# VectorE turns one more unit, xD of the first x is made from SBUF alone, and the loads of x and T are cut and ordered differently

## The chip, the cores and the metric

The kernel runs on one core of a Trainium2 chip. The metric is the device time of one execution in microseconds. Of the kernel before there are three timed runs, at 103.55, 103.83 and 106.04 us, with a median of 103.83 us, and one profiled execution at 103.36 us.

## The reference

```python
def reference(x, itok_B_1_98, L0_cond_T):       # x: 8 x 512 x 512, T: 100 x 512 x 512, float32
    def _L0_cond_ref(x, fwd_steps, T):
        Tb = T[fwd_steps - 1]                    # one matrix of T for each of the 8 batches
        return jnp.einsum('bij,bjk->bik', Tb, x)
    x = x + _L0_cond_ref(x, itok_B_1_98, L0_cond_T)
    return x
```

For each of eight batches one matrix of a table T is picked by a token, a float32 product of 512 x 512 x 512 is formed, and x is added.

## The kernel before, in words

**Units.** A batch is cut into N = 4 units of 128 output rows; unit U is batch U // 4, block U % 4. There are 32 units. For each unit TensorE needs the block of T transposed (its weights), and it multiplies it with all of x of the batch (four matmuls with 512 moving columns for each product).

**Three products.** To keep float32 accuracy with the type fp32r, x and T are split. xH is x rounded (ScalarE), xL = x - xH, and xD = xH - 4096 xL. TH is T / 4096 rounded, TL = T - 4096 TH and TD = TH - TL. A unit takes `multiply_high` (TH times xH into the bank `same`), `multiply_low` (TL times xL into the same bank) and `multiply_diff` (TD times xD into the bank `diff`, which ScalarE has filled before from `same`, called `seed`). VectorE then subtracts `diff` from x (`sum_up`). So a unit is 12 matmuls of 512 columns.

**Who makes what.** ScalarE makes xH (L213; L201 for the first x), TH (`cut_T`, L234; `cut_T_pair`, L241), the seeds (L249), and a copy of xH in PSUM, `xH_copy` (L219), from which VectorE makes xD (L353), so that VectorE reads one SBUF and one PSUM tensor there. VectorE makes xL of the first x (L339), all TL (L370 for unit 0, L376, L382), xD, and the sums (L390). GpSimd makes all TD (L312, L320) and xL of every later half x (L304). Turning (transposing) a block of T is done by TensorE for units 0 to 3 (`BY_PE = N`; L435, L446), as four transposes of 128 x 128, and by VectorE from unit 4 on (L360). VectorE's transpose only works within 32 x 32 quadrants, so T for these units is loaded in four pieces of 64 KB for each block (`load_T`, L160), which puts the quadrants in their places; the blocks that TensorE turns are loaded as they are (L156).

**The order.** It is written out by hand, a list for each engine, and semaphores tie the lists together. After the first units come steps k = 1 to 15, a step being two units: TensorE does high 2k, low 2k, diff 2k-1, high 2k+1, low 2k+1, diff 2k. In step k VectorE turns units 2k+2 and 2k+3 (for k > 1), makes xD of half x number k+1, sums up unit 2k-1, makes TL of pair k+1, and sums up unit 2k. ScalarE in a step: a seed, xH of half k+2, TH of pair k+1, a seed, `xH_copy`. GpSimd: xL of half k+2, TD of pair k+1.

**The loads.** Issued by SyncE (queue SP): T of batch 0 in three DMAs (blocks 0, 1, and 2 with 3 together), the first half of the second x (L148), then, once the tokens have landed in SBUF, blocks 0 and 1 of T of batch 1 in eight DMAs, the other half of the second x, the other eight DMAs of T of batch 1, and T of batch 2. ScalarE's queue carries the first x in three DMAs, the tokens, from the third x on whole x of 1 MB (L144, one in every second step), and the stores (L165).

**Around the start.** TensorE first multiplies with an identity matrix (L426, L428) until the first block of T is there. All waits of later work are on counts of semaphores, such as `TL_ready`, `xD_ready`, `turned_by_pe`.

## Time and profile before

| | |
|---|---|
| profiled execution | 103.36 us |
| its span, first to last instruction | 101.6 us |
| median of the three timed runs | 103.83 us |
| granted TensorE clock | 1.00 of full speed, in every slice |
| TensorE busy | 96.5 us, 95% of the span |
| VectorE busy | 87.0 us, 86% |
| GpSimd busy | 72.6 us, 71% |
| ScalarE busy | 65.3 us, 64% |
| DMA queue of SP, of ScalarE | 37.1% and 41.6% of 16 engines' span |

Busy time of TensorE counts matmuls, which overlap each other; the chain that ended last tells better what the end hangs on. The first 20 us, where the engines start one after another, are where the lists differ from the steady steps.

### The profile page before, as it was taken

The numbers are of one execution on the slowest core, as the hardware profiler recorded it, in microseconds if no ns is written. First come the engines' busy times: TensorE is split into PE (matmuls) and PEld (weight loads), VectorE is DVE, ScalarE is ACT, GpSimd is POOL, SyncE is SP. The second block draws the span as 40 slices with busy tenths as digits, with TensorE's granted clock in tenths as the row PEclk, the third lists the DMA queues.
The fourth block names the chain that finished last, engine by engine and source line by source line (L and its number), as shares of the span: only waits on it lengthen the run. The fifth ranks groups of instructions, "written<-read, shape, count | busy, mean of one in ns | idle before, by whom it ended". The sixth has DMA issues, their size and how long they took to land.

```text
span 101.6 us, 1827 instructions
## 1 busy us (share of the span) xinstructions
PE 96.5 (95%) x440; PEld 80.7 (79%) x440; DVE 87.0 (86%) x101; ACT 65.3 (64%) x87; POOL 72.6 (71%) x38
## 2 busy tenths in 40 slices
PE   3999999999999999999999999999999999999950
PEld 3997888888888888888888888888888888888840
DVE  0075989999999999999999999999999999993250
ACT  0766588758596876858585858596876858362100
POOL 2001369999979797988979797979797988908100
PEclk9999999999999999999999999999999999999999
DMA  1989996999999787998999899998989630405064
GB/s 46 306 219 416 276 282 131 319 283 335 343 329 322 238 252 238 336 315 244 292 364 300 213 324 313 246 323 219 357 272 335 213 126 26 181 3 206 6 275 138
DMA packets 20749, 25.30 MB, mean 249 GB/s; under 512 B 2306, under 2 KB 16898, under 8 KB 19970
## 3 DMA queue, kind: packets, MB, share of 16 engines
q10 hardware_dynamic: 3602, 15.34, 41.6%
q1 hardware_dynamic: 17136, 9.84, 37.1%
q8 instruction: 4, 0.07, 0.3%
q14 instruction: 7, 0.06, 0.2%
HBM read 16.78 MB, written 8.39 MB: 248 GB/s over the span
## 4 chain that ended last, share of the span: by engine, by line
PE 94%; DVE 1%; POOL 1%; issue 0%; POOLq 0%
PE same L461 29%; PE same L472 29%; PE diff L483 28%; PE diff L426 4%; PE same L428 3%; PE turned L446 1%; DVE out_sb L417 1%; DVE out_sb L390 1%; PE turned L435 0%; POOL eye L298 0%; POOL eye L296 0%; PE same L435 0%; POOLq L298 0%; POOLq L523 0%
## 5 line engine op out<-in xcount | busy, mean ns | idle before, releaser
L304 POOL TENSOR_TENSOR xL<-x_sb,xH 128x1024 fp32r<-128x1024 f32 x14 | 33.7, 2409 | 7.2 <-ACT xH L213 7.2
L320 POOL TENSOR_TENSOR TD_r<-TH_r,TL 128x1024 fp32r<-128x1024 f32 x14 | 33.7, 2407 | 2.9 <-issue 2.9
L472 PE MATMUL same<-xL,TL 128*128 128x512 f32 x128 | 34.4, 391 | 0.0
L461 PE MATMUL same<-xH,TH_r 128*128 128x512 f32 x128 | 34.4, 390 | 0.0
L483 PE MATMUL diff<-xD,TD_r 128*128 128x512 f32 x124 | 33.1, 389 | 0.0
L249 ACT ACTIVATE diff<-same 128x512 f32<-128x512 f32 x31 | 18.1, 583 | 22.3 <-PE same L472 22.1
L360 DVE STREAM_TRANSPOSE turned<-T_sb 128x512 f32<-128x512 f32 x28 | 29.3, 1090 | 0.2
L461 PEld LDWEIGHTS same<-xH,TH_r 128*128 128x128 f32 x128 | 23.9, 188 | 5.3 <-ACT TH_r L234 0.2
L472 PEld LDWEIGHTS same<-xL,TL 128*128 128x128 f32 x128 | 23.9, 188 | 4.9
L483 PEld LDWEIGHTS diff<-xD,TD_r 128*128 128x128 f32 x124 | 23.3, 188 | 4.8
L390 DVE TENSOR_TENSOR out_sb<-x_sb,diff 128x512 f32<-128x512 f32 x31 | 20.8, 671 | 4.0 <-PE diff L483 4.0
L353 DVE SCALAR_TENSOR_TENSOR xD<-xL,xH_copy 128x1024 fp32r<-128x1024 f32 x15 | 18.0, 1201 | 0.6 <-ACT xH_copy L219 0.6
L382 DVE SCALAR_TENSOR_TENSOR TL<-TH_r,turned 128x1024 fp32r<-128x1024 f32 x14 | 16.9, 1210 | 0.0
L219 ACT ACTIVATE xH_copy<-xH 128x1024 f32<-128x1024 f32 x15 | 15.4, 1024 | 0.0
L213 ACT ACTIVATE xH<-x_sb 128x1024 fp32r<-128x1024 f32 x14 | 14.8, 1055 | 0.3 <-DMA x_sb<-x 0.3
L241 ACT ACTIVATE TH_r<-turned 128x1024 fp32r<-128x1024 f32 x14 | 14.3, 1021 | 0.5 <-POOL TD_r L320 0.5
L312 POOL TENSOR_TENSOR TD_r<-TH_r,TL 128x512 fp32r<-128x512 f32 x4 | 5.2, 1294 | 10.7 <-DVE TL L370 8.4
L339 DVE TENSOR_TENSOR xL<-x_sb,xH 128x512 fp32r<-128x512 f32 x4 | 2.7, 690 | 5.6 <-ACT xH L201 5.5
L426 PE MATMUL diff<-eye 128*128 128x128 f32 x16 | 3.8, 431 | 1.5 <-POOL eye L298 1.5
L426 PEld LDWEIGHTS diff<-eye 128*128 128x128 f32 x16 | 3.5, 330 | 1.5 <-POOL eye L298 1.5
L428 PEld LDWEIGHTS same<-eye 128*128 128x128 f32 x20 | 3.4, 263 | 0.0
L428 PE MATMUL same<-eye 128*128 128x128 f32 x20 | 3.3, 341 | 0.0
(29 smaller groups left out, 20.7 us busy)
## 6 DMA issues: line engine op xcount, KB each, us to landing
out<-out_sb ACTq DMA_DIRECT2D x15, 512.0 KB, 5.9
T_sb<-T SPq DMA_DIRECT2D x112, 64.0 KB, 4.2
x_sb<-x ACTq DMA_DIRECT2D x6, 1024.0 KB, 7.4
x_sb<-x SPq DMA_DIRECT2D x2, 512.0 KB, 7.1
x_sb<-x ACTq DMA_DIRECT2D x2, 256.0 KB, 3.7
x_sb<-x ACTq DMA_DIRECT2D x1, 512.0 KB, 4.6
T_sb<-T SPq DMA_DIRECT2D x2, 256.0 KB, 5.5
T_sb<-T SPq DMA_DIRECT2D x1, 512.0 KB, 6.5
```

What stands on the lines that cost most here:

```text
L213: nc.scalar.activation(half(xH, h), x_sb[b % X_SLOTS][:, i:i + 2], COPY, scale=LEAN).then_inc(xH_ready, 2)
L219: nc.scalar.activation(xH_copy[:], half(xH, h).bitcast(fp32), COPY).then_inc(xH_copied, 1)
L249: nc.scalar.activation(diff[U % 2][:], same[U % 2][:], COPY, scale=-(RADIX + 1.0)).then_inc(seeded, 1)
L304: nc.gpsimd.tensor_tensor(half(xL, h), x_sb[b % X_SLOTS][:, i:i + 2], half(xH, h).bitcast(fp32), ALU.subtract).then_inc(xL_ready, 2)
L320: nc.gpsimd.tensor_tensor(TD_r[s][:], TH_r[s][:].bitcast(fp32), TL[s][:].bitcast(fp32), ALU.subtract).then_inc(TD_ready, 2)
L353: nc.vector.scalar_tensor_tensor(half(xD, h), half(xL, h).bitcast(fp32), -RADIX, high, ALU.mult, ALU.add).then_inc(xD_ready, 2)
L360: nc.vector.transpose(turned[:, U % 2].rearrange("p u (m q) -> p m u q", q=Q), T_sb[b % T_SLOTS][:, n].rearrange("p (m c u) -> p m u c", c ...
L382: nc.vector.scalar_tensor_tensor(TL[s][:], TH_r[s][:].bitcast(fp32), -RADIX, turned[:], ALU.mult, ALU.add).then_inc(TL_ready, 2)
L390: nc.vector.tensor_tensor(out_sb[b % OUT_SLOTS][:, n], x_sb[b % X_SLOTS][:, n], diff[U % 2][:], ALU.subtract).then_inc(sum_ready, 1)
L461: nc.tensor.matmul(same[U % 2][:], TH_r[p][:, i, j], xH[s][:, j], start=(j == 0), stop=False)
L472: done = nc.tensor.matmul(same[U % 2][:], TL[p][:, i, j], xL[s][:, j], start=False, stop=(j == N - 1))
L483: done = nc.tensor.matmul(diff[U % 2][:], TD_r[p][:, i, j], xD[s][:, j], start=False, stop=(j == N - 1), skip_group_check=True)
```

## The change

- `BY_PE` goes from 4 to 3: unit 3 is turned by VectorE (`turn(3)`), no longer by TensorE. TensorE's transposes of unit 2 now stand before `multiply_high(1)`.
- Block 3 of T of batch 0 is therefore loaded in four pieces of 64 KB; blocks 0, 1 and 2 are three DMAs of 256 KB.
- VectorE makes xD of the first x from xL and xH, both in SBUF, in three instructions (blocks 0, 1, and 2 with 3), the first two between its xL. ScalarE no longer copies xH of half 0 to PSUM.
- GpSimd's first TD also waits until all of the first xD is made.
- VectorE sums up unit 0 before it turns unit 5.
- x from the third on is loaded by halves of 512 KB, one in each step, with a semaphore for each half of a slot.
- The four pieces of a block of T are issued in the order 0, 2, 1, 3.

```diff
-    BY_PE = N
+    BY_PE = N - 1
...
             if b == 0:
-                return {0: (1, 1), 1: (2, 1), 2: (N, 1)}
+                return {0: (1, 1), 1: (2, 1), 2: (3, 1), 3: (N, G)}
             return {n: (n + 1, G) for n in range(N)}
...
-        def load_x(eng, b):
-            eng.dma_start(x_sb[b % X_SLOTS][:], x_part[b]).then_inc(x_loaded[b % X_SLOTS], 16)
-
-        def load_second_x(eng, i):
-
-            eng.dma_start(x_sb[1][:, 2 * i:2 * i + 2], x_part[1, :, 2 * i:2 * i + 2]).then_inc(half_x_loaded[i], 16)
+        def load_x_half(eng, h):
+            b, i = h // 2, h % 2
+            eng.dma_start(x_sb[b % X_SLOTS][:, 2 * i:2 * i + 2], x_part[b, :, 2 * i:2 * i + 2]
+                          ).then_inc(half_x_loaded[b % X_SLOTS][i], 16)
...
-                for g in range(G):
+                for g in [0, 2, 1, 3]:
...
             cut_first_T()
-            copy_xH_half(0)
             cut_T(1)
...
-            load_x(act, 2)
+            load_x_half(act, 4)
             for k in range(1, PAIRS):
...
-                if k % 2 == 0 and b + 2 < B:
+                if k + 4 < 2 * B:
                     if b >= 2:
                         act.wait_ge(sum_ready, (b - 1) * N)
-                    load_x(act, b + 2)
+                    load_x_half(act, k + 4)
...
                 pool.wait_ge(TL_ready, U + 1)
-                if U == 1:
-
-                    pool.wait_ge(xD_ready, N)
+
+                pool.wait_ge(xD_ready, N)
...
+            def first_xD(u, end):
+                dve.wait_ge(xH_ready, end)
+                dve.wait_ge(first_xL_ready, end)
+                nc.vector.scalar_tensor_tensor(xD[0][:, u:end], xL[0][:, u:end].bitcast(fp32), -RADIX,
+                                               xH[0][:, u:end].bitcast(fp32), ALU.mult, ALU.add).then_inc(xD_ready, end - u)
...
-            for u in range(N):
-                first_xL(u)
+            first_xL(0)
+            first_xL(1)
+            first_xD(0, 1)
+            first_xL(2)
+            first_xL(3)
+            first_xD(1, 2)
             cut_first_T()
-            cut_x_half(0)
+            first_xD(2, 4)
             cut_T(1)
-            cut_x_half(1)
+            turn(3)
             cut_T(2)
             turn(4)
             cut_T(3)
+            sum_up(0)
             turn(5)
-            sum_up(0)
...
             multiply_low(0)
+            turn(2)
             multiply_high(1)
-            turn(2)
-            turn(3)
             multiply_low(1)
```

Three places show what moves. The first is TensorE, from the first product of unit 0 to the first `multiply_diff`. L461 (L457 in the changed kernel) is `multiply_high`, L446 (L442) a turn, L472 (L468) `multiply_low`, L483 (L479) `multiply_diff`. Before:

```order
L461 MATMUL same<-xH,TH_r 128x512 x4
L446 MATMUL turned<-eye,T_sb 128x128 x4
L472 MATMUL same<-xL,TL 128x512 x4
L461 MATMUL same<-xH,TH_r 128x512 x4
L446 MATMUL turned<-eye,T_sb 128x128 x8
L472 MATMUL same<-xL,TL 128x512 x4
L483 MATMUL diff<-xD,TD_r 128x512 x4
```

Changed (here with the semaphores that an instruction waits for):

```order
L457 MATMUL same<-xH,TH_r 128x512 [waits xH_ready,first_TH_ready] x2
L457 MATMUL same<-xH,TH_r 128x512 [waits xH_ready,TH_ready] x2
L442 MATMUL turned<-eye,T_sb 128x128 [waits TL_ready,T_loaded0_1]
L442 MATMUL turned<-eye,T_sb 128x128 x3
L468 MATMUL same<-xL,TL 128x512 [waits first_xL_ready,TL_ready]
L468 MATMUL same<-xL,TL 128x512 [waits first_xL_ready] x3
L442 MATMUL turned<-eye,T_sb 128x128 [waits TL_ready,T_loaded0_2]
L442 MATMUL turned<-eye,T_sb 128x128 x3
L457 MATMUL same<-xH,TH_r 128x512 [waits TH_ready] x4
L468 MATMUL same<-xL,TL 128x512 [waits TL_ready]
L468 MATMUL same<-xL,TL 128x512 x3
L479 MATMUL diff<-xD,TD_r 128x512 [waits xD_ready,TD_ready,seeded]
```

Four of the twelve transposes behind unit 0 are gone, and the four of unit 2 stand one product earlier.

The second place is VectorE at the start. Before:

```order
L339 TENSOR_TENSOR xL0<-x_sb0,xH0 128x512 [waits xH_ready] x4
L370 SCALAR_TENSOR_TENSOR TL0<-TH_r0,turned 128x128 [waits first_TH_ready]
L370 SCALAR_TENSOR_TENSOR TL0<-TH_r0,same1 128x128 [waits first_TH_ready]
L370 SCALAR_TENSOR_TENSOR TL0<-TH_r0,turned 128x256 [waits TH_ready]
L353 SCALAR_TENSOR_TENSOR xD0<-xL0,xH_copy 128x1024 [waits xH_copied,first_xL_ready]
L376 SCALAR_TENSOR_TENSOR TL0<-TH_r0,turned 128x512 [waits TH_ready]
L353 SCALAR_TENSOR_TENSOR xD0<-xL0,xH0 128x1024 [waits first_xL_ready]
L376 SCALAR_TENSOR_TENSOR TL1<-TH_r1,turned 128x512 [waits TH_ready]
L360 STREAM_TRANSPOSE turned<-T_sb1 128x4x4x32 [waits TL_ready,T_loaded1_0]
```

Changed:

```order
L331 TENSOR_TENSOR xL0<-x_sb0,xH0 128x512 [waits xH_ready] x2
L337 SCALAR_TENSOR_TENSOR xD0<-xL0,xH0 128x512 [waits first_xL_ready,xH_ready]
L331 TENSOR_TENSOR xL0<-x_sb0,xH0 128x512 [waits xH_ready] x2
L337 SCALAR_TENSOR_TENSOR xD0<-xL0,xH0 128x512 [waits first_xL_ready,xH_ready]
L362 SCALAR_TENSOR_TENSOR TL0<-TH_r0,turned 128x128 [waits first_TH_ready]
L362 SCALAR_TENSOR_TENSOR TL0<-TH_r0,same1 128x128 [waits first_TH_ready]
L362 SCALAR_TENSOR_TENSOR TL0<-TH_r0,turned 128x256 [waits TH_ready]
L337 SCALAR_TENSOR_TENSOR xD0<-xL0,xH0 128x1024 [waits first_xL_ready,xH_ready]
L368 SCALAR_TENSOR_TENSOR TL0<-TH_r0,turned 128x512 [waits TH_ready]
L352 STREAM_TRANSPOSE turned<-T_sb0 128x4x4x32 [waits TL_ready,T_loaded0_3]
L368 SCALAR_TENSOR_TENSOR TL1<-TH_r1,turned 128x512 [waits TH_ready]
L352 STREAM_TRANSPOSE turned<-T_sb1 128x4x4x32 [waits TL_ready,T_loaded1_0]
```

Half of xD now stands ahead of the first TL, none waits for ScalarE's copy, and one more transpose stands in front of that of unit 4.

The third place is the queue of SP at its start. Before:

```order
L156 DMA T_sb0<-T 128x512
L156 ISA
L156 DMA T_sb0<-T 128x1024
L148 DMA x_sb1<-x 128x1024
L170 TENSOR_LOAD itok_sb
L160 ISA x2
```

Changed (`TENSOR_LOAD` reads the token, `ISA` is arithmetic of the sequencer):

```order
L153 DMA T_sb0<-T 128x512
L157 ISA
L157 DMA T_sb0<-T 32x4x128
L157 ISA
L157 DMA T_sb0<-T 32x4x128
L157 ISA
L157 DMA T_sb0<-T 32x4x128
L157 ISA
L157 DMA T_sb0<-T 32x4x128
L144 DMA x_sb1<-x 128x1024
L167 TENSOR_LOAD itok_sb [waits itok_loaded]
L157 ISA x2
```

Four more DMAs stand in front of the second x and of all of T from batch 1 on.

## Rows read from the trace of the kernel before

**Rows 1.** The page, part 4: share of the span on the chain that ended last.
```profile
PE 94%; DVE 1%; POOL 1%; issue 0%; POOLq 0%
```

**Rows 2.** The chain of waits, 0 to 20 us: start us, us, engine, tile, line, count.
```profile
10.13 0.53 PE turned L446 x4
...
12.55 0.95 PE turned L446 x8
```

**Rows 3.** Timeline, the first units: start us, us, engine, line, operation, [idle before, releaser].
```profile
6.94 1.29 DVE L339 TENSOR_TENSOR xL<-x_sb,xH 128x512 fp32r<-128x512 f32 x2 [0.56 <-ACT xH L201]
...
8.91 0.29 DVE L370 SCALAR_TENSOR_TENSOR TL<-TH_r,turned 128x128 fp32r<-128x128 f32 x1 [0.67 <-ACT TH_r L227]
...
9.24 1.02 ACT L219 ACTIVATE xH_copy<-xH 128x1024 f32<-128x1024 f32 x1
9.38 0.42 DVE L370 SCALAR_TENSOR_TENSOR TL<-TH_r,turned 128x256 fp32r<-128x256 f32 x1
...
9.91 0.56 PEld L446 LDWEIGHTS turned<-eye,T_sb 128*128 128x128 f32 x4 [0.22 <-issue]
...
12.14 1.22 DVE L353 SCALAR_TENSOR_TENSOR xD<-xL,xH 128x1024 fp32r<-128x1024 f32 x1
...
13.50 1.30 POOL L312 TENSOR_TENSOR TD_r<-TH_r,TL 128x512 fp32r<-128x512 f32 x1 [2.33 <-DVE xD L353]
...
14.47 1.12 DVE L360 STREAM_TRANSPOSE turned<-T_sb 128x512 f32<-128x512 f32 x1
...
14.76 2.41 POOL L304 TENSOR_TENSOR xL<-x_sb,xH 128x1024 fp32r<-128x1024 f32 x1
```

**Rows 4.** Timeline of SP's queue, 0 to 26 us: when its DMAs were issued.
```profile
4.34 0.60 SPq L148 DMA_DIRECT2D x_sb<-x  x1
6.84 4.03 SPq L160 DMA_DIRECT2D T_sb<-T  x8
10.92 0.42 SPq L148 DMA_DIRECT2D x_sb<-x  x1
```

**Rows 5.** Waits of SP's queue.
```profile
SPq L170 <- DMA itok_sb<-itok: 0.8, 1, 0.8
```

**Rows 6.** SP's DMAs issued 4.2 to 5 and 10.9 to 11.3 us: KB, us to landing.
```profile
x_sb<-x SPq DMA_DIRECT2D x1, 512.0 KB, 8.4
...
x_sb<-x SPq DMA_DIRECT2D x1, 512.0 KB, 5.8
```

**Rows 7.** SP's T pieces issued 6.5 to 8.6 and 8.7 to 10.9 us.
```profile
T_sb<-T SPq DMA_DIRECT2D x4, 64.0 KB, 4.6
...
T_sb<-T SPq DMA_DIRECT2D x5, 64.0 KB, 3.6
```

**Rows 8.** The page, part 6: the later x, KB, median us to landing.
```profile
x_sb<-x ACTq DMA_DIRECT2D x6, 1024.0 KB, 7.4
```

**Rows 9.** Timeline, 16 to 27 us: the second x and the pairs behind it.
```profile
16.79 1.06 ACT L213 ACTIVATE xH<-x_sb 128x1024 fp32r<-128x1024 f32 x1 [0.28 <-DMA x_sb<-x]
...
18.39 2.41 POOL L304 TENSOR_TENSOR xL<-x_sb,xH 128x1024 fp32r<-128x1024 f32 x1
18.55 1.02 ACT L241 ACTIVATE TH_r<-turned 128x1024 fp32r<-128x1024 f32 x1
...
19.68 1.22 DVE L382 SCALAR_TENSOR_TENSOR TL<-TH_r,turned 128x1024 fp32r<-128x1024 f32 x1
...
20.77 1.28 POOL L312 TENSOR_TENSOR TD_r<-TH_r,TL 128x512 fp32r<-128x512 f32 x1
...
21.30 0.87 PEld L472 LDWEIGHTS same<-xL,TL 128*128 128x128 f32 x4
...
22.21 0.87 PEld L483 LDWEIGHTS diff<-xD,TD_r 128*128 128x128 f32 x4
...
25.20 1.22 DVE L382 SCALAR_TENSOR_TENSOR TL<-TH_r,turned 128x1024 fp32r<-128x1024 f32 x1
...
26.74 0.87 PEld L472 LDWEIGHTS same<-xL,TL 128*128 128x128 f32 x4
```

More of the change, by code:

```diff
@@ L70, in cond_resid @@
         itok_loaded = sem("itok_loaded")
-        x_loaded = [sem(f"x_loaded{s}") for s in range(X_SLOTS)]
+        half_x_loaded = [[sem(f"half_x_loaded{s}_{i}") for i in range(2)] for s in range(X_SLOTS)]
         first_x_loaded = [sem(f"first_x_loaded{i}") for i in range(len(FIRST_X))]
-        half_x_loaded = [sem(f"half_x_loaded{i}") for i in range(2)]
         T_loaded = [[sem(f"T_loaded{s}_{n}") for n in range(N)] for s in range(T_SLOTS)]
@@ L177, in _ @@
             load_T(sp, t, 0)
-            load_second_x(sp, 0)
+            load_x_half(sp, 2)
             sp.wait_ge(itok_loaded, 16)
@@ L181, in _ @@
             load_T(sp, t, 1, range(2))
-            load_second_x(sp, 1)
+            load_x_half(sp, 3)
             load_T(sp, t, 1, range(2, N))
@@ L204, in cut_x_half @@
                 b = h // 2
-                if b == 1:
-                    act.wait_ge(half_x_loaded[h % 2], 16)
-                else:
-                    act.wait_ge(x_loaded[b % X_SLOTS], 16 * ((b - 2) // X_SLOTS + 1))
+                act.wait_ge(half_x_loaded[b % X_SLOTS][h % 2], 16 * (b // X_SLOTS + (1 if b % X_SLOTS else 0)))
                 if b >= X_SETS:
@@ L216, in copy_xH_half @@
                 act.wait_ge(xH_ready, 2 * h + 2)
-                if h:
-                    act.wait_ge(xD_ready, 2 * h)
+                act.wait_ge(xD_ready, 2 * h)
                 nc.scalar.activation(xH_copy[:], half(xH, h).bitcast(fp32), COPY).then_inc(xH_copied, 1)
@@ L340, in first_xL @@
                                         ).then_inc(first_xL_ready, 1)
-            def cut_x_half(h):
-                if h < 2:
-                    dve.wait_ge(first_xL_ready, 2 * h + 2)
-                else:
-                    dve.wait_ge(xL_ready, 2 * h - N + 2)
-                if h != 1:
-                    dve.wait_ge(xH_copied, max(h, 1))
+            def first_xD(u, end):
[3 more added lines that the diff above has]
+                                               xH[0][:, u:end].bitcast(fp32), ALU.mult, ALU.add).then_inc(xD_ready, end - u)
+            def cut_x_half(h):
+                dve.wait_ge(xL_ready, 2 * h - N + 2)
+                dve.wait_ge(xH_copied, h - 1)
                 if h // 2 >= X_SETS:
                     dve.wait_ge(diff_ready, (h // 2 - X_SETS + 1) * N)
-                high = half(xH, h).bitcast(fp32) if h == 1 else xH_copy[:]
-                nc.vector.scalar_tensor_tensor(half(xD, h), half(xL, h).bitcast(fp32), -RADIX, high,
+                nc.vector.scalar_tensor_tensor(half(xD, h), half(xL, h).bitcast(fp32), -RADIX, xH_copy[:],
                                                ALU.mult, ALU.add).then_inc(xD_ready, 2)
```

## The prediction

> **What bounds the kernel now.** I read the page's part 4 first: 94% of the span lies on TensorE [rows 1], so time goes only where TensorE's chain gets shorter or gets a gap. Then the chain in order of time, from the first product on: behind unit 0 it is products and transposes without a gap, and the transposes stand in it with 0.53 us for four and 0.95 us for eight [rows 2]. Once the steps run, a product of four matmuls takes 0.91 us (21.30 to 22.21) and a step of two units 5.44 us (21.30 to 26.74) [rows 9]. Third, the timeline of the first 27 us, to see how close the other engines are behind TensorE. They are close. TL of the pair that begins at 19.68 is ready at 20.90, and TensorE loads it at 21.30, so 0.40 us of slack. TD of unit 3 is ready at 22.05 and loaded at 22.21: 0.16 us. TL of the next pair is ready at 26.42 and loaded at 26.74: 0.32 us [rows 9]. VectorE needs 5.52 us from one pair's TL to the next (19.68 to 25.20) [rows 9], that is, it has nothing to spare against TensorE's 5.44: what it is late at the start stays. So the gain on TensorE counts only as far as VectorE and GpSimd follow within these slacks.
>
> **The change part by part.**
>
> *Transposes of unit 3 leave TensorE.* Half of the eight: 0.95 / 2 = 0.47 us off the chain, no more than that, since nothing else on TensorE changes. Moving unit 2's transposes ahead of `multiply_high(1)` costs nothing and gives ScalarE's TH of unit 1 more time. The row for this price is that of the chain, 0.12 us for each transpose. The Trainium skill (TensorE: Matmul & The Clock Gate, Part 4: PE-mode transpose) puts a transpose at about 275 ns in a kernel's context, which as an estimate would make the gain 4 x 0.275 = 1.1 us; the chain shows 0.12 us, because consecutive transposes overlap, and the measurement decides.
>
> *VectorE's start.* Two xD instructions of 512 columns come in between the xL. Nearest rows: an xL of that width is 1.29 / 2 = 0.65 us, and the xD of twice the width is 1.22 us [rows 3], so 0.65 us each. The first fits in the idle 0.56 us ahead of 6.94, the second in the 0.67 us ahead of 8.91 [rows 3], each with up to 0.1 us left over. The first TL piece starts about 0.1 us later, and TensorE's transposes of unit 1 wait for the last of them (0.42 us from 9.38, then 0.22 us of idle at TensorE before 9.91) [rows 3]. Cost on the chain: 0.1 us (bounds 0 and 0.2). The remaining xD of 1.22 us ends at about 9.9 + 1.2 = 11.1.
>
> *ScalarE's copy goes*, 1.02 us [rows 3], beside the chain. It moves nothing by itself, since what follows it waits for TensorE.
>
> *GpSimd.* TD of unit 0 now waits for the xD, so it runs 11.1 to 12.4 (1.30 us each [rows 3]) and TD of unit 1 to 13.7, where it ended at 14.80 before, held back by an xD that VectorE made at 12.14 [rows 3]. `multiply_diff(0)` comes at 12.55 + 0.95 + 0.91 = 14.4 before and about 14.0 now, so the later TD of unit 0 is covered by 1.6 us. GpSimd is free for xL of the second x 1.1 us earlier than 14.76.
>
> *VectorE turns unit 3*: 1.12 us more [rows 3], after TL of unit 1. From 11.1: TL of unit 1 to 12.0, the turn to 13.1, TL of unit 2 to 13.8, so the turn of unit 4 could begin at 13.8 instead of 14.47 [rows 3]. But its T arrives later, see next. I take 14.3. The sum of unit 0 ahead of the turn of unit 5 lets ScalarE's seed of unit 2 go without a wait; it changes no total.
>
> *The queue of SP.* Four DMAs more at 4.03 / 8 = 0.50 us each [rows 4]. The second x's first half is issued at 4.34 + 2.0 = 6.35. Before, 1.90 us lay between the end of that issue (4.94) and 6.84, of which 0.8 us were the wait for the tokens [rows 4, 5], which have landed by 6.95 now; so the pieces of T of batch 1 start at 6.95 + 1.1 = 8.05, 1.2 us later, and so does the second half of x, at 12.1. A latency of 4.6 us [rows 7] puts the last piece of unit 4's block (issued at 9.6) at 14.2.
> When do the halves of x land? Not before their old times, 4.34 + 8.4 = 12.7 and 10.92 + 5.8 = 16.7, since the same bytes stand ahead in the queue; not after the old latencies from the new issues, 14.75 and 17.9 [rows 4, 6]. The latency of T's pieces fell from 4.6 to 3.6 us while the queue drained [rows 7]: a later issue meets a shorter queue. I take 13.3 for the first (8.4 us is mostly queue) and 17.2 for the second (5.8 us is less so).
> The first half at 13.3 gives xH at 14.4, and GpSimd starts its xL 0.3 us before the old 14.76: harmless.
> The second half at 17.2 is the term that counts. xH is made 17.3 to 18.3, a seed of 0.5 us follows (in the trace before, xH ended at 17.85 and TH of the pair began at 18.55, with a wait in between [rows 9]), TH of the pair 18.8 to 19.9, TL from 19.9 instead of 19.68: VectorE 0.2 us late. GpSimd's xL of that half starts at 18.4 as before, and TD of unit 3 again ends at 22.05 [rows 9].
>
> *x by halves from the third x on.* Before, 1 MB landed 7.4 us after its issue [rows 8]. Each half is issued two steps, some 10.9 us, before ScalarE cuts it; cover 3.5 us, cost nothing. Six or seven more issues lie on ScalarE's queue, beside its instructions. *The order 0, 2, 1, 3* of pieces that are waited for together: nothing; if it disturbed the DMA engines, the same cover pays.
>
> **The sum.** TensorE gains 0.47 - 0.1 = 0.37 us up to the first steps. Then it meets what did not get earlier: TD of unit 3 at 22.05 against 22.21 - 0.37 = 21.84 is a gap of 0.2 us, and TL of the second pair, 26.42 + 0.2 = 26.62 against 26.74 - 0.37 = 26.37, makes it 0.25 us in all. What stays is 0.1 to 0.2 us, 0.15. On the profiled execution that is 103.36 - 0.15 = 103.2. This execution is 0.47 us below the median of the runs (one of them stands apart at 106.04); the mean of it and the two lower runs is 103.58, and the forecast of the timed median is 103.58 - 0.15 = 103.4.
>
> **The rivals.**
>
> *The whole gain arrives.* If the second half of x lands by 16.8, all of ScalarE and VectorE is on time or earlier (VectorE had 0.6 us in hand at unit 4), and TensorE keeps 0.4 to 0.47 us: 103.1. For it: the bytes ahead in the queue are the same. Against: T's pieces need SP's issue, at 0.50 us for 64 KB.
>
> *The loads of x come too late: slower.* With the old latency of 5.8 us the second half lands at 17.9; xH to 19.1, TH from 19.6 to 20.6, TL from 20.6, 0.95 us behind the old 19.68. TensorE had 0.32 us in hand for it, so the whole kernel is 0.63 us later than before: 103.58 + 0.6 = 104.2. The point from which it decides: with TL more than 0.32 us late, that is x later than 17.3, the kernel is slower than before. If the first half also keeps its 8.4 us, it lands at 14.75, xH ends at 15.9, GpSimd is 1.1 us late, less its slack of 0.16: 104.5. For it: four more DMAs stand in front. Against: the queue was emptying. The Trainium skill (DMA: Bandwidth & Descriptors, the table of measured HBM-to-SBUF transfers) speaks for this rival: it has 138 GB/s at 64 KB against 341 GB/s at 1 MB, which for a block of 256 KB would be an estimated 1.1 us more, and it advises batches of 1 MB.
>
> *Nothing arrives.* VectorE, not TensorE, becomes the clock, because its 5.5 us of a step is what counts once TensorE waits for TL: between 0 and 0.15 us of gain is lost again, 103.6.
>
> *Several at once*, or T of unit 5 late too, in front of all of VectorE's list: over 2 us slower, above 105.7; no row points to it.
>
> **How the numbers follow.** Chances: forecast 0.50, whole gain 0.21, x late 0.20, nothing arrives 0.05, several at once 0.03, and 0.01 for a gain above 2 us, which no row allows (TensorE gives up 0.47 us of work). 2% of the time, about what a measurement of this kernel can tell from no change, is 2.1 us, so all of the first four are "within": 0.96; faster 0.01; slower 0.03. The range takes in the whole gain with the spread between runs (103.1 - 0.2 = 102.9) and most of the late x (104.3); the forecast's own range is 103.1 to 103.7.
>
> **What would show it.** Right: 8 transposes L442 instead of 12; the first part of the chain 0.3 to 0.4 us shorter up to `multiply_diff(0)`; a gap of about 0.2 us of TensorE before TD of unit 3 or TL of a pair between 20 and 27 us; the second half of x at ScalarE at 17.0 to 17.4. The wait of ScalarE for that half, 0.28 us before [rows 9], longer. Wrong: a TensorE with no gap and an end 0.45 us earlier, or ScalarE waiting a microsecond for x and a chain that goes through it.

## The result, and the profile after

The changed kernel is slower: a median of 104.51 us in 13 runs (103.65 to 105.32) against 103.82 us in 13 runs of the kernel before (103.33 to 106.04), a ratio of 1.0061 with a 95% interval of 1.0036 to 1.0087. The forecast was 103.4 us with a range to 104.3. One of its rivals, the loads of x that come too late, gave 104.2 us by the mechanism that is the nearest to what happened. Ratios, here and in the experiments, compare the runs that lie within about 1.5% of the fastest of the same kernel. The profiled execution took 104.61 us, with a span of 102.5 us against 101.6.

The page, part 4, of the changed kernel: the chain that ended last is no longer TensorE's alone.

```profile
PE 75%; SPq 9%; DMA 6%; issue 2%; ACT 2%; DVE 2%; ACTq 0%; DVEq 0%
```

Before, 94% of it was TensorE [rows 1]. Here is the piece where it leaves TensorE, from the chain in order of time, 0 to 24 us (start us, us, what; SPq is the queue of SP, a DMA's time is that from issue to landing):

```profile
11.65 0.32 SPq L157
11.97 0.05 issue
12.02 6.09 DMA x_sb<-x
18.15 0.04 issue
18.19 0.41 ACT xH L208
...
19.19 0.55 ACT diff L243
19.74 0.95 ACT TH_r L235
20.74 0.04 issue
20.79 1.23 DVE TL L374
22.02 0.04 issue
22.06 1.19 PE same L468 x4
```

Read from the bottom: TensorE waits for TL of the second pair, VectorE for ScalarE's TH, ScalarE was held by xH of the second x's second half, that by its DMA, and the DMA by SP's issues. SP's queue, from the timeline (start us, us, count):

```profile
4.45 2.08 SPq L157 DMA_DIRECT2D T_sb<-T  x4
...
6.58 0.42 SPq L144 DMA_DIRECT2D x_sb<-x  x1
...
8.14 3.83 SPq L157 DMA_DIRECT2D T_sb<-T  x8
...
12.02 0.42 SPq L144 DMA_DIRECT2D x_sb<-x  x1
```

These stand 2.2, 1.3 and 1.1 us later than in [rows 4], as forecast. What they did to the engines, from the timeline, 9 to 27 us ([idle before, releaser] at the end):

```profile
9.94 1.22 DVE L337 SCALAR_TENSOR_TENSOR xD<-xL,xH 128x1024 fp32r<-128x1024 f32 x1
10.14 0.56 PEld L442 LDWEIGHTS turned<-eye,T_sb 128*128 128x128 f32 x4 [0.22 <-issue]
...
11.31 2.56 POOL L304 TENSOR_TENSOR TD_r<-TH_r,TL 128x512 fp32r<-128x512 f32 x2 [9.83 <-DVE xD L337]
...
12.35 1.12 DVE L352 STREAM_TRANSPOSE turned<-T_sb 128x512 f32<-128x512 f32 x1
...
14.98 1.13 DVE L352 STREAM_TRANSPOSE turned<-T_sb 128x512 f32<-128x512 f32 x1 [0.94 <-DMA T_sb<-T]
15.04 2.41 POOL L297 TENSOR_TENSOR xL<-x_sb,xH 128x1024 fp32r<-128x1024 f32 x1 [1.18 <-ACT xH L208]
...
18.19 1.06 ACT L208 ACTIVATE xH<-x_sb 128x1024 fp32r<-128x1024 f32 x1 [1.38 <-DMA x_sb<-x]
...
19.40 2.40 POOL L297 TENSOR_TENSOR xL<-x_sb,xH 128x1024 fp32r<-128x1024 f32 x1 [0.70 <-DVE xD L345]
19.68 1.00 ACT L235 ACTIVATE TH_r<-turned 128x1024 fp32r<-128x1024 f32 x1
19.79 0.76 PEld L479 LDWEIGHTS diff<-xD,TD_r 128*128 128x128 f32 x4 [0.64 <-ACT diff L243]
...
20.75 0.76 PEld L457 LDWEIGHTS same<-xH,TH_r 128*128 128x128 f32 x4 [0.21 <-issue]
20.79 1.22 DVE L374 SCALAR_TENSOR_TENSOR TL<-TH_r,turned 128x1024 fp32r<-128x1024 f32 x1 [0.81 <-ACT TH_r L235]
...
22.06 0.76 PEld L468 LDWEIGHTS same<-xL,TL 128*128 128x128 f32 x4 [0.55 <-DVE TL L374]
...
23.16 0.76 PEld L479 LDWEIGHTS diff<-xD,TD_r 128*128 128x128 f32 x4 [0.34 <-issue]
...
26.24 1.22 DVE L374 SCALAR_TENSOR_TENSOR TL<-TH_r,turned 128x1024 fp32r<-128x1024 f32 x1
```

Against [rows 9]: xH of the second half begins at 18.19 instead of 16.79, TL of the second pair at 20.79 instead of 19.68, TensorE loads it at 22.06 instead of 21.30. Four gaps of TensorE (0.64, 0.21, 0.55, 0.34 us of weight-load idle) take back the 0.47 us and more. From there on the two run in step: the next pair's TL is at 26.24 instead of 25.20, the span ends 0.9 us later.

Not all of these 0.9 us belong to the change, since TensorE's first product also begins later. Its first and last weight loads behind the identity matrix, before:

```profile
8.92 0.77 PEld L461 LDWEIGHTS same<-xH,TH_r 128*128 128x128 f32 x4 [0.19 <-ACT TH_r L227]
...
97.23 0.55 PEld L493 LDWEIGHTS same<-xD,TD_r 128*128 128x128 f32 x4
```

and in the changed kernel:

```profile
9.15 0.77 PEld L457 LDWEIGHTS same<-xH,TH_r 128*128 128x128 f32 x4 [0.20 <-ACT TH_r L221]
...
98.11 0.55 PEld L489 LDWEIGHTS same<-xD,TD_r 128*128 128x128 f32 x4
```

The first product begins between 8.74 and 9.79 us in the profiles of this document, in changed and unchanged kernels alike, so 0.23 us of the difference is scatter. From the first product to the last weights it is 88.31 us before and 88.96 after, 0.65 us more. This stretch is used below to compare single profiles.

What the DMA engines did meanwhile shows in windows. Those of the kernel before (the last three columns: granted clock, mean busy share of the 16 DMA engines, which can exceed 1 where transfers overlap, GB/s):

```profile
8.00:10.00 2.00, 2.00 (x13) 1.47 (x12) 1.13 (x4) 1.41 (x4) 0.12 (x1) 1.00 1.04 426
...
16.00:18.00 2.00, 2.00 (x11) 1.65 (x10) 1.90 (x4) 1.57 (x2) 2.00 (x2) 1.00 0.49 111
8.00:16.00 8.00, 8.00 (x44) 6.58 (x44) 6.29 (x10) 5.80 (x11) 3.79 (x3) 1.00 1.08 308
```

and of the changed one:

```profile
8.00:10.00 2.00, 1.89 (x11) 1.31 (x9) 1.64 (x6) 0.74 (x3) 0.00 (x0) 1.00 1.14 286
...
16.00:18.00 2.00, 2.00 (x10) 1.68 (x9) 2.00 (x4) 0.81 (x1) 2.00 (x2) 1.00 1.16 219
8.00:16.00 8.00, 7.89 (x40) 6.33 (x39) 6.20 (x10) 4.59 (x10) 3.52 (x3) 1.00 1.13 263
```

The engines are busy from 8 to 16 us in both, but deliver 308 GB/s before and 263 after. Before, they have caught up by 16 to 18 us (share 0.49); after, they have not (1.16). The issues differ as well as the sizes, so these rates alone do not say which of the two lowered them.

### The profile page after: what moved, and what is told of

The parts are those of the page before. It is cut to its first block, busy times and chain, and to the rows that moved or that the text cites. A ratio compares the mean times of both kernels' runs of the same rounds, so it can differ in the third digit from the quotient of the medians.

```text
span 102.5 us, 1843 instructions
## 1 busy us (share of the span) xinstructions
PE 96.9 (95%) x436; PEld 80.0 (78%) x436; DVE 87.8 (86%) x103; ACT 64.2 (63%) x86; POOL 73.0 (71%) x38
## 4 chain that ended last, share of the span: by engine, by line
PE 75%; SPq 9%; DMA 6%; issue 2%; ACT 2%; DVE 2%; ACTq 0%; DVEq 0%
PE same L468 25%; PE diff L479 25%; PE same L457 24%; DMA x_sb<-x 6%; SPq L157 5%; SPq L167 2%; SPq L153 2%; DVE TL L374 1%; ACT TH_r L235 1%; PE diff L489 1%; ACT diff L243 1%; PE same L489 0%; SPq L144 0%; DVE out_sb L413 0%; ACT xH L208 0%
## 5 line engine op out<-in xcount | busy, mean ns | idle before, releaser
L468 PE MATMUL same<-xL,TL 128*128 128x512 f32 x128 | 34.5, 391 | 0.1
L457 PE MATMUL same<-xH,TH_r 128*128 128x512 f32 x128 | 34.5, 392 | 0.0
L479 PE MATMUL diff<-xD,TD_r 128*128 128x512 f32 x124 | 33.4, 391 | 0.2 <-ACT diff L243 0.2
L352 DVE STREAM_TRANSPOSE turned<-T_sb 128x512 f32<-128x512 f32 x29 | 30.6, 1103 | 1.0 <-DMA T_sb<-T 0.9
L468 PEld LDWEIGHTS same<-xL,TL 128*128 128x128 f32 x128 | 23.9, 188 | 5.4 <-DVE TL L374 0.5
L457 PEld LDWEIGHTS same<-xH,TH_r 128*128 128x128 f32 x128 | 23.8, 188 | 5.2 <-issue 0.2
L479 PEld LDWEIGHTS diff<-xD,TD_r 128*128 128x128 f32 x124 | 23.1, 188 | 5.7 <-ACT diff L243 0.6
L382 DVE TENSOR_TENSOR out_sb<-x_sb,diff 128x512 f32<-128x512 f32 x31 | 21.4, 691 | 3.9 <-PE diff L479 3.9
L374 DVE SCALAR_TENSOR_TENSOR TL<-TH_r,turned 128x1024 fp32r<-128x1024 f32 x14 | 17.2, 1229 | 0.8 <-ACT TH_r L235 0.8
L345 DVE SCALAR_TENSOR_TENSOR xD<-xL,xH_copy 128x1024 fp32r<-128x1024 f32 x14 | 17.1, 1222 | 0.0
L235 ACT ACTIVATE TH_r<-turned 128x1024 fp32r<-128x1024 f32 x14 | 14.3, 1020 | 0.6 <-POOL TD_r L312 0.6
L213 ACT ACTIVATE xH_copy<-xH 128x1024 f32<-128x1024 f32 x14 | 14.3, 1023 | 0.0
```

Of the source, the lines that this page charges most:

```text
L235: nc.scalar.activation(TH_r[p % T_SETS][:], turned[:], COPY, scale=LEAN / RADIX).then_inc(TH_ready, 2)
L345: nc.vector.scalar_tensor_tensor(half(xD, h), half(xL, h).bitcast(fp32), -RADIX, xH_copy[:], ALU.mult, ALU.add).then_inc(xD_ready, 2)
L352: nc.vector.transpose(turned[:, U % 2].rearrange("p u (m q) -> p m u q", q=Q), T_sb[b % T_SLOTS][:, n].rearrange("p (m c u) -> p m u c", c ...
L374: nc.vector.scalar_tensor_tensor(TL[s][:], TH_r[s][:].bitcast(fp32), -RADIX, turned[:], ALU.mult, ALU.add).then_inc(TL_ready, 2)
L382: nc.vector.tensor_tensor(out_sb[b % OUT_SLOTS][:, n], x_sb[b % X_SLOTS][:, n], diff[U % 2][:], ALU.subtract).then_inc(sum_ready, 1)
L457: nc.tensor.matmul(same[U % 2][:], TH_r[p][:, i, j], xH[s][:, j], start=(j == 0), stop=False)
```

## The experiments

Each was timed against the kernel before on the same chip; the groups ran on different chips, so a ratio of one group set against one of another is less certain than within a group. Theory A: the four added DMAs make the second x late. Theory B: VectorE's longer list at the start holds TensorE. Theory C: the later halves of x or the order of the pieces disturb the whole run. Theory D came after the first two groups: it is what the DMA engines deliver, not SP's issue.

**Which part carries the loss.** The first run takes the part on unit 3 out of the change, the second does it alone.

```diff
# a1_unit3_back, on the changed kernel; TensorE's turn(3) behind multiply_high(1)
-    BY_PE = N - 1
+    BY_PE = N
-                return {0: (1, 1), 1: (2, 1), 2: (3, 1), 3: (N, G)}
+                return {0: (1, 1), 1: (2, 1), 2: (N, 1)}
-            turn(3)              # VectorE
# a2_unit3_alone, on the kernel before: the same lines the other way round
```

> The changed kernel with unit 3 turned by TensorE again (T of batch 0 in three DMAs, the last of 512 KB; eight transposes on TensorE behind unit 0), all else as changed. Theory A (the four added DMAs ahead of the second x make its second half land at 18.1 instead of 16.7, and ScalarE, which waits for it in order, makes everything behind it late): the second half lands at 16.6 to 16.9 again, TensorE has no gap between 19 and 24 us, and the time is that of before, ratio 0.997 to 1.001. Theory B (VectorE's list at the start is too long: xD from SBUF in three instructions, the sum before the turn): TL of the second pair begins later than 19.8 though x is in time, ratio 1.003 or more. Theory C (the later x by halves, or the order of the pieces, disturbs the DMA engines for the whole run): ratio 1.004 or more, with gaps behind 30 us.

> The kernel before with this part alone: unit 3 turned by VectorE, its block loaded in four pieces of 64 KB. Theory A: the whole loss is here, the second half of the second x lands at about 18, ScalarE waits 1.2 to 1.5 us for it, TL of the second pair begins at 20.6 to 20.9, ratio 1.004 to 1.009. Theory B: the loss needs the changed xD; ratio 0.998 to 1.002. Theory C: the same as B.

Measured: 0.9999 (0.9964 to 1.0035) without the part, 1.0060 (1.0015 to 1.0106) with it alone. So the whole loss belongs to the part on unit 3, and for xD from SBUF, the halves of the later x, the order of the pieces and of the sum together nothing is measured. Theory C falls, and B in the form that blames the new xD. In the profile of a2, ScalarE waits for the second half until 18.84 and VectorE's TL of the second pair begins at 21.43, later than the 20.6 to 20.9 expected. One caution: in a1's profile ScalarE waited for that half until 17.52, not the 16.6 to 16.9 expected. Single landings scatter by more than half a microsecond from one execution to the next, so one landing proves little and the timed runs have to be weighed with it.

**The added DMAs by themselves**, on the kernel before, TensorE turning unit 3 as ever:

```diff
# a4_four_plain (a5_four_small: the first line only, so runs of 512 bytes)
+                return {0: (1, 1), 1: (2, 1), 2: (3, 1), 3: (N, G)}
+                if b == 0:
+                    for g in range(G):
+                        eng.dma_start(T_sb[s][g * Q:(g + 1) * Q, n:end], T_rows[bass.ds(t, 1), g * Q:(g + 1) * Q, n:end]...
```

> The kernel before, TensorE turns unit 3, but T of batch 0 goes in three DMAs of 256 KB and, for block 3, four of 64 KB with whole rows of 2 KB (no small packets). It separates the number of DMAs that SP issues from the size of their packets. If the issue time of SP is the cause (0.50 us each, second half of x issued 1.1 us later): it lands at 17.8 to 18.1, ratio 1.004 to 1.008. If the packets of 512 bytes are the cause: it lands at 16.7 to 17.2, ratio 0.999 to 1.003.

> As the run with four plain DMAs, but block 3 goes in the four pieces with runs of 512 bytes that VectorE's transpose would need, while TensorE still turns it, so the rows of unit 3 of batch 0 are not the reference's. If the issue time is the cause: the same as with plain rows, 1.004 to 1.008. If the small packets are: the second half lands at about 18.1 here and not there, ratio 1.005 to 1.010 here alone. Theory B expects 0.998 to 1.002 for both.

Measured: 1.0100 (1.0053 to 1.0147) and 1.0102 (1.0064 to 1.0141). The four DMAs cost 1.0 us with no change in any engine's work, more than the 1.004 to 1.008 that issue time alone was expected to cost, and the length of the runs in them makes no difference that these intervals show. The part alone, which has these DMAs and 0.47 us of transposes less, is at 1.0060: the difference, 0.4%, fits the price of the transposes, within intervals that overlap. Windows of a4, 8 to 16 us:

```profile
8.00:16.00 8.00, 7.68 (x39) 6.26 (x40) 5.53 (x9) 5.47 (x11) 3.41 (x3) 1.00 1.11 248
```

248 GB/s at a busy share of 1.11: the engines are full and deliver less than before. The second half lands at 18.3 and ScalarE waits 1.43 us for it. In its profile a second wait appears, of ScalarE for the third x (1.1 us, near 25 us), which is still one DMA of 1 MB there and was issued late. In a5's profile the second x happened to be in time (xH at 16.71) and VectorE waited for T's pieces twice instead, 0.44 us before 43.96 and 0.47 us before 55.42. So the toll isn't always taken at the same place.

**Four ways to bring the second x forward.**

```diff
# b1_x_on_scalar_queue, on the changed kernel (b2: the second one ahead of cut_T(1); b4: b1 on the kernel before)
-            load_x_half(sp, 2)   ...   load_x_half(sp, 3)
             for u in range(N):
                 cut_first_x(u)
+            load_x_half(act, 2)
             cut_first_T()
             cut_T(1)
+            load_x_half(act, 3)
# b3_swapped_on_sp, on the changed kernel
-            load_T(sp, t, 1, range(2))
+            load_T(sp, t, 1, range(1))
             load_x_half(sp, 3)
+            load_T(sp, t, 1, range(1, 2))
```

> The changed kernel, but both halves of the second x are issued by ScalarE (the first behind its four xH of the first x, at about 7.5 us, the second behind TH of unit 1, at about 11.5), so SP's queue carries T alone and its pieces start 0.4 to 0.9 us earlier. Theory A (late loads behind SP's four added issues are the whole loss, the transposes are a gain of 0.4 us): x in time, TensorE without a gap from 12 to 30 us, ratio to before 0.993 to 0.998. Theory B (VectorE's longer list at the start is what holds TensorE): the gap between 19 and 24 us stays although x landed before 17, ratio 1.003 or more.

> As the run before, with the second half of the second x issued by ScalarE two instructions earlier, behind TH of unit 0 (about 9.6 us). Theory A: x lands by 15.5, but T of unit 4 and 5, which share the DMA engines, land 0.3 to 1 us later than there; ratio 0.993 to 0.999. Theory B: 1.003 or more, as there.

> The changed kernel, but SP issues the second half of the second x ahead of T's block 1 of batch 1 instead of behind it, four issues (2 us) earlier, nothing else moved. Theory A: ScalarE's wait for x, 1.4 us in the changed kernel, is gone; T of unit 5 lands about 1 us later, at 17 to 17.5, against a turn of unit 5 that could start at 17.2; ratio 0.995 to 1.002. Theory B: 1.003 or more.

> The kernel before with its second x issued by ScalarE at the same two places, TensorE still turning unit 3. It tells what moving the loads is worth by itself. Theory A (the kernel before had its x just in time, with little to gain): ratio 0.996 to 1.001, and the changed kernel with x on ScalarE's queue lies 0.3% to 0.5% below this one, the transposes' worth. Theory B: this one is the faster of the two.

Measured: 1.0063 (1.0029 to 1.0098), 1.0083 (1.0038 to 1.0128), 1.0042 (0.9996 to 1.0088), 1.0023 (0.9985 to 1.0061). None brings the gain, against what theory A expected; the ratios are those that theory B expected (1.003 or more), and b4 came out as the faster of b1 and b4, as B had it. The profiles answer it. VectorE's lines of b1, and of b2:

```profile
15.11 1.11 DVE L352 STREAM_TRANSPOSE turned<-T_sb 128x512 f32<-128x512 f32 x1 [1.00 <-DMA T_sb<-T]
18.12 1.13 DVE L352 STREAM_TRANSPOSE turned<-T_sb 128x512 f32<-128x512 f32 x1 [0.74 <-DMA T_sb<-T]
```

```profile
15.61 1.14 DVE L352 STREAM_TRANSPOSE turned<-T_sb 128x512 f32<-128x512 f32 x1 [1.32 <-DMA T_sb<-T]
```

VectorE waits for T of units 4 and 5, in b2 for T of unit 4. In b2 the second half of x, issued at 9.29, is cut at 15.95 without a wait, and T is late in its place. In b1 both are late: the half was issued at 11.00, 1.0 us earlier than in the changed kernel, and ScalarE still waited for it until 17.86. So moving a load among queues did not make the loads as a whole arrive earlier. Theory A as "SP's order" falls; what these profiles support is that too little is delivered in the first 18 us.

**Issue time or delivery.**

```diff
# c1_after_old_T_load, on the changed kernel: T of batch 0 in three DMAs again
+                return {0: (1, 1), 1: (2, 1), 2: (N, 1)}
# c2_before_sp_waits, on the kernel before
+            sp.wait_ge(xH_ready, 3)
             load_second_x(sp, 0)
# c3_before_four_blocks, on the kernel before
+                return {0: (1, 1), 1: (2, 1), 2: (3, 1), 3: (N, 1)}
# c4_after_merged_blocks, on the changed kernel
+                return {0: (1, 1), 1: (3, 1), 3: (N, G)}
```

> The changed kernel with all its work (VectorE turns unit 3, xD from SBUF, later x by halves), but T of batch 0 loaded as before in three DMAs, so block 3 is not in the layout that VectorE's transpose needs and the rows of unit 3 of batch 0 are not the reference's. It takes the added DMAs away and keeps every instruction of the engines. Theory A and D (the loss is in the loads, whether through SP's issue or through what the DMA engines deliver): ratio 0.994 to 0.998, TensorE without a gap from 12 to 30 us. Theory B (VectorE's list): 1.002 or more.

> The kernel before, in which SP waits for the third xH of the first x (6.9 us) before it issues the second x's first half: everything behind it on SP is issued about 2.5 us later for that half and 1.2 to 1.5 us later for the rest, as in the changed kernel, but no DMA is added or cut. Theory A, issue time alone: ratio 1.005 to 1.010. Theory D, the DMA engines deliver the smaller pieces more slowly and the issue time only hides behind their queue: ratio 0.999 to 1.004.

> The kernel before with T of batch 0 in four DMAs of 256 KB (runs of 2 KB) in place of 256, 256 and 512 KB (runs of 4 KB in the last): one DMA more, no small one. Theory A: one issue of 0.5 us, 1.000 to 1.003. Theory D with the run length as its cause: block 3 and all behind it land 0.5 us or more later, 1.003 to 1.007.

> The changed kernel with blocks 1 and 2 of the first T in one DMA of 512 KB (runs of 4 KB), so one DMA fewer on SP than in the changed kernel. Block 1 lands later, at about 10.2 instead of 9.5, where TensorE wants it at 9.9. Theory A: everything behind it 0.5 us earlier, ratio 1.000 to 1.005, less what TensorE waits for block 1. Theory D: the second half of x 0.5 to 0.8 us earlier than in the changed kernel, ratio 0.998 to 1.003.

Measured: c1 1.0032 (1.0001 to 1.0064), c2 1.0157 (1.0083 to 1.0232; six runs), c3 0.9995 (0.9961 to 1.0028), c4 1.0056 (1.0016 to 1.0097). c3: one more DMA, with shorter rows, is free, so it is the four of 64 KB that cost. c4, with one DMA fewer than the changed kernel, was expected to be at 1.005 at most and is not faster: in its profile TensorE waits for block 1, which comes in the larger DMA, and turns unit 1 about 0.4 us later after its first product (9.19 to 10.56) than the changed kernel does (9.15 to 10.14). That may hide what the missing DMA gives. c2 was a coarser test than meant: SP went on only at 7.65 us, 3.3 us late and not 2.5, and issued the second half at 13.04. Yet that half was there at 17.42, after 4.3 us (row below), against 6.1 us in the changed kernel from 12.02. The DMA engines' busy share was 0.83 from 8 to 16 us there, so the queue had drained, as the prediction assumed. Issue time alone therefore costs when it is large (1.6% for 2.1 to 3.3 us). What it costs in the change, where the engines stay full (1.13) and the issues are 1.1 to 2.2 us later, no run shows apart from the delivery.

```profile
x_sb<-x SPq DMA_DIRECT2D x1, 512.0 KB, 4.3
```

c1 gave back half of the loss and no gain. That misses what theories A and D expected (0.994 to 0.998) and is what theory B expected (1.002 or more). Its profile, whose span is 101.7 us, has TensorE without a gap up to 64 us and then this (TensorE, and VectorE's wait behind it):

```profile
64.78 0.77 PEld L468 LDWEIGHTS same<-xL,TL 128*128 128x128 f32 x4 [0.62 <-DVE TL L374]
```

```profile
60.77 1.12 DVE L352 STREAM_TRANSPOSE turned<-T_sb 128x512 f32<-128x512 f32 x1 [0.51 <-DMA T_sb<-T]
```

So VectorE's list, which is the changed kernel's, held TensorE nowhere by itself: the gain was there for 55 us and was lost by one late piece of T.

**Light loads of T.** The last six are about DMA work; five take some of it away. A light batch comes in four DMAs of 256 KB with whole rows instead of sixteen pieces of 64 KB, with the same bytes and the same work of the engines. The rows then lie as VectorE's transpose cannot use them, so these kernels leave out a right result for the units named in the expectations; they tell only about time.

```diff
# d1_before_light_T, d2_after_light_T (with T of batch 0 in three DMAs), d3_after_light_T_four_pieces
-            return {n: (n + 1, G) for n in range(N)}
+            return {n: (n + 1, 1) for n in range(N)}
# h1_after_light_T1, on the changed kernel
+            return {n: (n + 1, 1 if b == 1 else G) for n in range(N)}
# g1_unit3_alone_old_T_load: a2 with T of batch 0 in three DMAs
# h2_before_swapped: b3's edit on the kernel before
```

> The kernel before with T of batches 1 to 7 loaded in four DMAs of 256 KB each, whole rows, instead of sixteen pieces of 64 KB: the layout is not what VectorE's transpose needs, so units 4 to 31 are not the reference's, but every instruction of the engines stays. It takes away SP's many issues and the small packets. If T's pieces cost the kernel before anything, ratio 0.990 to 0.998; if not, 0.998 to 1.001.

> The changed kernel with the same light loads of T for batches 1 to 7 and T of batch 0 in three DMAs as before (unit 3 and units 4 to 31 not the reference's). Theory D (the loads of T take the gain of the transposes back anywhere in the run): this kernel is 0.3 to 0.5% faster than the light version of the kernel before, TensorE has no gap from 12 us to the end. Theory B (VectorE's longer list eats it): the two are equal within 0.15%, or this one is slower.

> As the run before, but with block 3 of batch 0 in its four pieces (only units 4 to 31 not the reference's). What stands behind them on SP is light, eight DMAs to unit 11 instead of 32. Theory A (the four issues delay the second half of x, whatever comes behind): that half lands about 1.5 us later than in the run before and the kernel is 0.3 to 0.8% slower than it. Theory D: with four DMAs for a batch there is room, the half of x lands before 16.9, and the two differ by under 0.2%.

> The kernel before with VectorE turning unit 3 and nothing else changed, T of batch 0 in its three DMAs (unit 3 of batch 0 not the reference's). Theory D: as the changed kernel with the old load, 1.000 to 1.004, with waits of VectorE for T here and there. Theory B with the new xD or the order of the sum at fault: 0.994 to 0.998 here, where these are as before. If the halves of x and the order of the pieces matter in the middle of the run: also below 1.000.

> The changed kernel with T of batch 1 alone in four DMAs of 256 KB, whole rows (units 4 to 7 not the reference's), all other loads and all instructions of the engines as changed; the four pieces of block 3 of batch 0 stay. SP issues the second half of the second x about 2.9 us earlier. If the loss sits around the second x at the start: ratio 0.995 to 0.998, like the version with light T throughout (0.9950). If T's stream takes it anywhere in the run: 1.001 to 1.004.

> The kernel before, but SP issues the second half of the second x ahead of T's block 1 of batch 1, two microseconds earlier; nothing is added. In the profiles of this kernel's relatives ScalarE waits 0.3 to 1.0 us for that half. If that wait costs time in the kernel before, ratio 0.995 to 0.998; if its cover holds there or T of unit 5, now later, takes its place, 0.999 to 1.003.

Measured: d1 0.9975 (0.9938 to 1.0012), d2 0.9991 (0.9956 to 1.0026), d3 0.9950 (0.9911 to 0.9989), g1 1.0027 (0.9982 to 1.0071), h1 0.9937 (0.9905 to 0.9969), h2 0.9972 (0.9938 to 1.0007).

h1 is the changed kernel, four added DMAs and all, and only T of batch 1 is light: from 1.0061 to 0.9937 (on two chips), about 1.2% of the time, clearly faster than the kernel before and a little below the 0.995 expected. So the loss sits where T of batch 1 is loaded, in the first 20 us. Its windows, 8 to 16 us, and its timeline there:

```profile
8.00:16.00 8.00, 7.66 (x38) 6.27 (x39) 6.99 (x12) 5.55 (x11) 4.59 (x3) 1.00 1.05 329
```

```profile
9.00 0.42 SPq L144 DMA_DIRECT2D x_sb<-x  x1
...
15.66 1.07 ACT L208 ACTIVATE xH<-x_sb 128x1024 fp32r<-128x1024 f32 x1
...
19.02 1.20 DVE L374 SCALAR_TENSOR_TENSOR TL<-TH_r,turned 128x1024 fp32r<-128x1024 f32 x1
...
20.95 0.87 PEld L468 LDWEIGHTS same<-xL,TL 128*128 128x128 f32 x4
```

329 GB/s; ScalarE never waits for the second x, VectorE is 0.66 us ahead of [rows 9], and TensorE loads the second pair's TL at 20.95, 0.35 us earlier than the 21.30 there, though its first product began 0.17 us later. The stretch from the first product to the last weights, in h1 and in d2:

```profile
9.09 0.77 PEld L457 LDWEIGHTS same<-xH,TH_r 128*128 128x128 f32 x4 [0.20 <-ACT TH_r L221]
...
96.88 0.55 PEld L489 LDWEIGHTS same<-xD,TD_r 128*128 128x128 f32 x4
```

```profile
9.42 0.77 PEld L457 LDWEIGHTS same<-xH,TH_r 128*128 128x128 f32 x4 [0.20 <-ACT TH_r L221]
...
97.21 0.55 PEld L489 LDWEIGHTS same<-xD,TD_r 128*128 128x128 f32 x4
```

| kernel | unit 3 turned by | stretch, us |
|---|---|---|
| before, c3, b4, d1, a1 | TensorE | 88.31, 88.33, 88.34, 88.34, 88.27 |
| h1, d2 | VectorE | 87.79, 87.79 |
| c1 | VectorE, one wait for T | 88.40 |
| changed kernel | VectorE, late x | 88.96 |

In the kernels of the first two rows no load holds TensorE behind its first product. Between these rows lie 0.52 us, the transposes. h1 and d2 have every engine's list of the changed kernel, VectorE's too, so theory B falls: that list holds TensorE nowhere when the loads are in time. By d1's profile light loads alone take nothing off TensorE's stretch in the kernel before. What was not run is the kernel before with T of batch 1 alone light, so in the timed 0.9937 the share of the light load is not measured; d1, its nearest relative, is at 0.9975. h1 also shifts x's issue to 9.00 us, so it frees issue slots and DMA time at once, and does not say how much each gives. d3 is of the same kind and agrees. In the timed runs d2 was expected to beat d1 by 0.3 to 0.5% and does not (0.9991 and 0.9975, intervals overlapping), which is what theory B expected of that pair: the timed runs do not resolve the 0.52 us that the two profiles show. Why d3, with four DMAs more than d2, was the faster one is open; it may be scatter.

g1, like c1, shows no gain where only the four DMAs were taken away; in its profile ScalarE waited until 17.76 for x, and TensorE has gaps at 19.55 and 21.81. So the four DMAs are not the whole account. Without them the gain of 0.52 us still does not arrive in the timed runs, and only single profiles say why (a late piece of T in c1, a late x in g1). Both are 0.3% above the kernel before with intervals that nearly or just touch 1. h2 points to a small gain in the kernel before, which isn't shown, since its interval includes 1. No version with the reference's result was shown to beat the kernel before.

## Why the prediction was wrong

**The base.** The forecast stood on 103.58 us, from three executions; 13 runs of the kernel before have a median of 103.82. That is 0.24 of the 1.1 us by which it missed. The change itself was forecast at -0.15 us and measured at +0.7.

**The transposes: right in size.** From the first product to the first `multiply_diff` TensorE takes 4.59 us (9.15 to 13.74) instead of 5.12 (8.92 to 14.04), 0.53 us less; 0.47 was forecast, and the 0.1 us subtracted for a later TL did not appear (0.99 us from the first product to the turn of unit 1 in both). The gapless stretches differ by 0.52 us, and a2 against a4 and a5 gives about 0.4%. The 1.1 us that, as an estimate, the Trainium skill's figure of 275 ns would make of it (TensorE: Matmul & The Clock Gate, Part 4: PE-mode transpose) appears nowhere.

**VectorE's start, GpSimd, ScalarE's copy: right within 0.35 us.** The xD of 512 columns fitted in the gaps, xD was complete at 9.94 + 1.22 = 11.2 (forecast 11.1), GpSimd's two TD ran from 11.31 to 13.87 (forecast 11.1 to 13.7), the turn of unit 3 began at 12.35 (forecast 12.0). The turn of unit 4 was forecast for 14.3 and came at 14.98, with a wait of 0.94 us for T.

**The queue of SP: issue right, landing wrong. This is the step that failed.** "[...] a later issue meets a shorter queue. I take [...] 17.2 for the second (5.8 us is less so)." The issue came at 12.02 as worked out (12.1), but the latency rose to 6.1 us instead of falling to 5.1, and the half was there at 18.1, even behind the bound of 17.9 that the old latency gave. Of the 1.4 us by which it landed later than before, 1.1 are the later issue, which a shorter queue was to hide in part, and 0.3 a longer latency. The first half, too, came 0.5 us behind its forecast (6.58 + 7.2 = 13.8 for 13.3). The bound was no bound: it held the latency of [rows 6] fixed while the change put four DMAs in front, with the engines full and delivering less (286 instead of 426 GB/s at 8 to 10 us, 263 instead of 308 at 8 to 16). The fall of T's latency in [rows 7] was read as an emptying queue, but in the kernel before the DMA share was above 1 through all of 8 to 16 us, a window that was not looked at for this step. c2 agrees with the rule where nothing is added (4.3 us, with the engines at 0.83). Chance had its part in the single profile: with the four DMAs in front ScalarE began on that half at 16.71 in a5 and 16.70 in c4, but at 18.38 in a4 and 18.84 in a2, and the forecast of 17.2 lies inside that scatter; a5 and c4 are slower in the timed runs all the same (1.0102, 1.0056). How the loss divides between the later issue and the lower rate stays open.

The sentence on the Trainium skill (DMA: Bandwidth & Descriptors, the table of measured transfers), by which small transfers go at a lower rate and a block would take an estimated 1.1 us more, pointed the right way. That table is of transfers over 128 partitions issued from GpSimd, and the pieces here go over 32 partitions from SP's queue. Its 1.1 us have no counterpart in a row here: of the 1.4 us of added delay 1.1 are SP's later issue. a4 shows only that such pieces cost, 1.0%.

**What the lateness costs: undersized for one more reason.** The prediction priced TL and TD behind ScalarE's wait. It named the seed in between, but not who waits for it: `multiply_diff` of unit 2 stood for ScalarE's seed, 0.64 us at 19.79, the largest of the four gaps. TD of unit 3, forecast to end at 22.05 as before, ended at 23.05 (21.76 + 1.29), behind GpSimd's xL of the late half, which began at 19.40 and not at the 18.4 of the forecast. The rule that TL more than 0.32 us late makes the kernel slower held: counted from the first product TL was 0.88 us late (20.79 - 9.15 against 19.68 - 8.92), less 0.32 leaves 0.56 us, and the stretch to the last weights grew by 0.65 us, the timed median by 0.69.

**The later halves of x and the order of the pieces: right**, nothing measured in a1.

**The sign of being wrong came.** The prediction named "ScalarE waiting a microsecond for x and a chain that goes through it": ScalarE waited 1.38 us, and the chain above goes through it. Its rival for this gave 104.2 from the wrong base; 103.82 + 0.6 would be 104.4, beside the measured 104.51. The 104.5 that it gave with the first half late is near by luck, since that half came at 13.8 and not at 14.75.

**The size of the cover in the middle of the run: overrated.** The range's upper end, 104.3, was set by one late landing in an otherwise quiet stream. Waits for T's pieces at 28 to 61 us in several profiles (a5, b3, c1, c4) show that the stream has moments without slack well behind the start.

## What to carry to other kernels

Where DMA engines are near full, price a new transfer by what the engines deliver and not by its issue alone or by an old latency: take the DMA share and rate over the stretch in which the data is due, and see where the engines fall idle; only that idle time (here 16 to 18 us, gone after the change) is slack. A gain of 0.5 us on the busiest engine is worth nothing if it is paid for by making a load slower that everything in order behind it waits for. And test a suspected load by lightening its neighbours: bringing the late transfer forward only moved the wait to another one. Compare single profiles by a stretch inside them, here from the first product to the last, since the start alone scattered by 1 us, and lay the control beside the test: the kernel before with the same light load was not run.

## What the runs showed that was not expected

- Four DMAs of 64 KB over 32 partitions each, in place of half of one of 512 KB, cost 1.0% of the kernel whether their runs are 2 KB (1.0100) or 512 bytes (1.0102). One of 256 KB more costs nothing (0.9995).
- The latency of the same 512 KB, issued by the same queue, was 4.3 us in c2, where the engines' share was 0.83, and 6.1 us in the changed kernel (1.13), with 5.8 and 8.4 us in the kernel before. In a5, with the changed kernel's issues, it was 4.6 us, so the queue does not fix it alone.
- The trace has 16 completions for such a DMA. In the kernel before, 15 of them had come by 15.39 us for the second x's second half and the last at 16.71; in a4 the last two both came at 18.29. The old landing, from which the prediction took its latency, hung on one late part.
- The landing of the second x's second half scatters between executions by 0.5 us or more (ScalarE began at 16.66 in c1, 17.52 in a1 and 17.76 in g1, all three issued between 10.7 and 11.0 us), in kernels whose instructions last the same within some hundredths of a microsecond. That is why a single profile of a start like this one can't be taken for the median.
